# Weights by column blocks, token ids by one small matmul, and a setup order rewritten

## The chip, the cores and the metric

The kernel runs on one core of a Trainium2 chip, in float32. The metric is the device time of one launch in microseconds (us), as the median of several runs. TensorE (PE) multiplies, VectorE (DVE) and ScalarE (ACT) move and convert, GpSimd (POOL) selects small tables and issues gathers, SyncE (SP) issues the plain transfers.

## What is computed

`x` is [64, 64, 512]: 64 tokens of 64 rows. Four stages follow each other, each added to its input. Token b picks its adapter in each stage by an id of its own.

```python
x = x + x @ W_base.T + scaling[e0] * (((x @ Wt.T) @ A0[e0].T) @ B0[e0].T) @ Wp.T    # e0: 4 adapters of rank 16
x = x + x @ W1.T     + scalings[e1] * ((x @ A1[e1].T) @ B1[e1].T)                   # e1: 8 adapters of rank 16
x = x + einsum('bct,bcd->bdt', x, w2[e2])                                            # e2: 8 matrices 64x64
x = x + einsum('bct,bcd->bdt', x, w3[e3])                                            # e3: 200 matrices 64x64
```

## The kernel before

**Two phases.** The setup (about the first 38 us) folds the weights of the first two stages into one 512x512 matrix `g01` and small tables. Then eight turns of four token pairs follow (`PAIRS` = 32, `QUAD` = 4, `QUADS` = 8). A turn multiplies w2 and w3 of its tokens (`token_mix`), applies the product to x (`mix`, result `y_ps`), reads it to `y_all` and splits it into a rounded float32r half and a remainder (`yy`), multiplies both with `g01` (`apply`, 12 matmuls for a pair), reduces to rank rows (`reduce`) and adds the adapters' part (`close`), which reads rows `v_sel` gathered from the HBM table `v_table`.

**The folding.** `g1` is (W1 + 1) transposed on PE: 16 transposes of 128x128 blocks of `w1_sb`, into four banks `g1_0` to `g1_3`. POOL first adds the unit matrix to each diagonal block (L353, and L348 for `wb_sb`, which is W_base). ACT reads each bank as a rounded high half, DVE subtracts it to get the low half (`low_g1`). W_base is split in the same way (`wb_high_k`, `wb_low_k`). `g01` sums over four k: step k needs `g1_k` and `wb_k`, high and low, and is 12 matmuls of 512 columns (4 high x high, 8 mixed); step 0 begins with its four high x high.

Between the steps stand the transposes of Wp (`wpT`), of A1, A0 and w2, the products `vu` (which need the 1 MB transfer of Wt), `gu1T`, `cross`, `v0g1` and four matmuls `v_0` to `v_3`, whose results DVE sums into `v_tab`. One SP transfer writes `v_tab` to `v_table`.

**Order.** Nothing is scheduled by a tool. Each engine has its list, written by hand, and waits on semaphores. `setup_ps`, `setup_act` and `setup_dve` count the finished setup steps of PE, ACT and DVE; `ORDER` names the PSUM bank of each PE result, `ACT_STEPS` and `DVE_STEPS` the order of the readers. An engine stands still behind a wait, with everything that its list has behind it. SP's list is one queue of transfers. `keep_warm(16)` is 16 transposes of the unit matrix into a bank that is not read.

**Token ids.** Ids e3, e0 and e1 are copied to all 128 partitions by transfers that repeat the row 128 times (`ids`), and e0, e1, e2 once more to one partition (`code_ids`). DVE makes gather rows for w3 (`find_w3_rows`), table rows (`find_v_rows`) and packed codes, six linked small operations.

Of the kernel before, what the change touches and what calls it, by code (L numbers as in the profile page):

```python
# [40 lines left out]
def build(nc, x, e0_ids, e1_ids, e2_ids, e3_ids, w_base, w_t, a0, b0, w_p, s0, w1, a1, b1, s1, w2, w3, out):  # L41
# [995 lines left out]
```

## Time and profile before

| | us |
|---|---|
| median of 3 runs | 172.2 (171.82 to 172.25) |
| the profiled execution | 172.37 |
| its span in the trace | 170.2 |
| PE busy | 163.6 (96% of the span) |
| DVE / POOL / ACT busy | 91.1 / 86.7 / 48.5 |
| TensorE clock granted, mean | 0.997 |

The span runs from the first to the last recorded event; 2.2 us of the execution lie outside it. A busy PE is not PE at its peak, since ends of matmuls are modelled: PE times below are differences of starts.

### The profile page before, as it was taken

What the parts mean: (1) busy time and instruction counts of PE and PEld (TensorE: products, weight loads), DVE (VectorE), ACT (ScalarE), POOL (GpSimd) and SP (SyncE); (2) the same over time, 40 slices, a digit from 0 to 9 for tenths busy, and PEclk for the clock granted to TensorE, in tenths of its full rate; (3) what the DMA queues carried; (4) which work ended last, traced back from release to release, by engine and by line L of the source; (5) the groups of instructions that cost most, each with busy time, mean ns of one, the idle gap of its engine ahead of it and who ended that gap; (6) DMA issues with size and microseconds to landing.
All of it is one profiled execution on the core that took longest, in us unless ns stands there. A gap on an engine that the chain in (4) does not pass through costs nothing.

```text
span 170.2 us, 6468 instructions
## 1 busy us (share of the span) xinstructions
PE 163.6 (96%) x2348; PEld 125.0 (73%) x2348; DVE 91.1 (54%) x212; ACT 48.5 (28%) x96; POOL 86.7 (51%) x194
## 2 busy tenths in 40 slices
PE   5889999999999999999999999999999999999992
PEld 5669467678786878687868886877778687868761
DVE  4195975899770846263636645563666180617010
ACT  3142426244230602240223024220503060214021
POOL 4410477764675648475737674756454053608200
PEclk9999999999999999999999999999999999999998
DMA  4799942119550594077309531953394059006406
GB/s 141 252 329 321 282 177 85 33 60 331 190 192 27 168 322 145 23 208 293 131 15 294 209 137 70 285 178 116 123 311 161 31 155 337 2 0 250 123 9 242
DMA packets 16614, 28.75 MB, mean 169 GB/s; under 512 B 3862, under 2 KB 3990, under 8 KB 16598
## 3 DMA queue, kind: packets, MB, share of 16 engines
q1 hardware_dynamic: 14294, 23.31, 41.8%
q0 software_dynamic: 2304, 5.25, 9.1%
q8 instruction: 8, 0.13, 0.3%
q14 instruction: 8, 0.07, 0.1%
HBM read 18.85 MB, written 9.70 MB: 168 GB/s over the span
## 4 chain that ended last, share of the span: by engine, by line
PE 91%; DMA 3%; DVE 1%; SPq 1%; issue 1%; ACT 1%; POOL 0%; DVEq 0%
PE o_ps L751 65%; PE y_ps L751 12%; PE z_ps L751 8%; DMA wb_sb<-in_L_cond_W_base_dram 3%; PE p_ps L751 3%; PE y_ps L764 1%; SPq L231 1%; PE y_ps L811 1%; DVE g L552 0%; PE p_ps L853 0%; DVE b_by L546 0%; ACT o_sb L486 0%; PE p_ps L824 0%; PE z_ps L811 0%; PE p_ps L811 0%
## 5 line engine op out<-in xcount | busy, mean ns | idle before, releaser
L751 PE MATMUL o_ps<-g,yy 128*128 128x512 f32 x384 | 92.1, 395 | 0.0
L751 PEld LDWEIGHTS o_ps<-g,yy 128*128 128x128 f32 x384 | 70.8, 188 | 16.1 <-issue 0.8
L339 POOL COPY u_sel<-u_tab 128x64 f32 x128 | 32.3, 258 | 41.3 <-PE z_ps L751 31.5
L318 POOL DMA_INDIRECT w_all<-in_L_cond_weights_dram,w_rows x32 | 31.8, 994 | 9.6 <-issue 9.6
L631 DVE COPY y_all<-y_ps 128x512 f32<-128x512 f32 x32 | 20.6, 686 | 15.0 <-PE y_ps L751 14.9
L673 DVE COPY o_sb<-o_ps 128x512 f32<-128x512 f32 x15 | 9.7, 687 | 34.5 <-PE o_ps L751 34.5
L426 ACT ACTIVATE yy<-y_all 128x512 fp32r<-128x512 f32 x32 | 19.7, 632 | 16.5 <-DVE y_all L631 16.1
L638 DVE TENSOR_TENSOR yy<-y_all,yy 128x512 fp32r<-128x512 f32 x32 | 21.2, 701 | 3.0 <-ACT yy L426 2.7
L327 POOL DMA_INDIRECT v_sel<-v_table,v_rows x16 | 17.5, 1094 | 6.2 <-issue 6.2
L445 ACT ACTIVATE o_sb<-o_ps 128x512 f32<-128x512 f32 x16 | 8.7, 595 | 37.9 <-PE o_ps L751 37.9
L751 PE MATMUL y_ps<-p_now,x_raw 64*64 64x64 f32 x1024 | 18.6, 221 | 0.0
L665 DVE COPY w_sel<-w2T 64x64 f32 x56 | 12.5, 222 | 10.6 <-issue 7.2
L751 PEld LDWEIGHTS y_ps<-p_now,x_raw 64*64 64x64 f32 x1024 | 16.4, 134 | 1.7 <-DVE v_tab L552 0.4
L751 PEld LDWEIGHTS z_ps<-y_all,u_sel 128*32 128x32 f32 x512 | 8.0, 109 | 9.0 <-issue 9.0
L439 ACT ACTIVATE z<-z_ps 128x64 f32<-128x64 f32 x16 | 3.6, 227 | 34.8 <-PE z_ps L751 34.8
L751 PE MATMUL o_ps<-g,wb 128*128 128x512 f32 x48 | 12.2, 400 | 1.0 <-ACT g L389 0.8
L751 PEld LDWEIGHTS o_ps<-g,wb 128*128 128x128 f32 x48 | 8.7, 188 | 4.1 <-ACT g L389 1.0
L751 PE MATMUL z_ps<-y_all,u_sel 128*32 128x64 f32 x512 | 10.5, 222 | 0.0
L751 PE MATMUL o_ps<-v_sel,z 32*64 32x512 f32 x128 | 8.9, 613 | 0.0
L348 POOL TENSOR_TENSOR wb_sb<-wb_sb,ident 128x128 f32<-128x128 f32 x4 | 2.1, 514 | 10.6 <-DMA wb_sb<-in_L_cond_W_base_dram 10.6
L792 PE MATMUL o_ps<-ident 128*128 128x128 f32 x16 | 3.7, 421 | 1.8 <-POOL ident L306 1.8
L432 ACT ACTIVATE p_now<-p_ps 128x256 f32<-128x256 f32 x8 | 3.1, 385 | 5.4 <-PE p_ps L751 5.3
(115 smaller groups left out, 104.5 us busy)
## 6 DMA issues: line engine op xcount, KB each, us to landing
x_raw<-in_x_dram SPq DMA_DIRECT2D x16, 512.0 KB, 4.7
out_dram<-o_sb SPq DMA_DIRECT2D x14, 512.0 KB, 5.4
w_sb<-in_L_cond_W_dram SPq DMA_DIRECT2D x4, 256.0 KB, 3.6
wb_sb<-in_L_cond_W_base_dram SPq DMA_DIRECT2D x4, 256.0 KB, 7.1
wp_sb<-in_L_cond_Wp_dram SPq DMA_DIRECT2D x2, 512.0 KB, 6.3
wt_sb<-in_L_cond_Wt_dram SPq DMA_DIRECT2D x1, 1024.0 KB, 8.9
v_table<-v_tab SPq DMA_DIRECT2D x1, 1024.0 KB, 5.7
out_dram<-o_sb SPq DMA_DIRECT2D x4, 256.0 KB, 2.3
```

The lines of the kernel that those rows point to most:

```text
L318: pool.indirect_dma_start(out=w3_all[:, j, :], out_offset=None, in_=w3_flat, in_offset=bass.IndirectOffsetOnAxis(ap=w3_rows[:, j:j + 1], a ...
L327: pool.indirect_dma_start(out=v_sel[:, h, :], out_offset=None, in_=v_table, in_offset=bass.IndirectOffsetOnAxis(ap=v_rows[:, h, i:i + 1], ...
L339: nc.gpsimd.tensor_copy(u_sel[u][:, :, b, RANK * part:RANK * part + RANK], u_tab[:, :, bass.ds(e, 1), :].rearrange("p k a r -> p k (a r)") ...
L426: nc.scalar.activation(yy[u][:, :, 0, :], y_all[u % 2][:, :, :], ACT.Copy).then_inc(yh_set, 1)
L439: nc.scalar.activation(z[:, h, :], z_ps[:, 0:SEQ], ACT.Copy).then_inc(z_set, 1)
L445: nc.scalar.activation(o_sb[:, u, :], o_ps[u][:, :], ACT.Copy).then_inc(o_set, 1)
L631: nc.vector.tensor_copy(y_all[u % 2][:, :, :].rearrange("p k (b t) -> p b k t", b=2), y_of(u)).then_inc(yf_set, 1)
L638: nc.vector.tensor_tensor(yy[u][:, :, 1, :], y_all[u % 2][:, :, :], yy[u][:, :, 0, :].bitcast(F32), ALU.subtract).then_inc(yl_set, 1)
L665: nc.vector.tensor_copy(to[rows, u, :], w2T[rows, bass.ds(g, 1), :].rearrange("p a c -> p (a c)")).then_inc(w2_placed, 1)
L673: nc.vector.tensor_copy(o_sb[:, u, :], o_ps[u][:, :]).then_inc(o_set_dve, 1)
L751: return nc.tensor.matmul(dst, lhsT, rhs, start=start, stop=stop)
L792: nc.tensor.transpose(o_ps[3][:, 0:PART], ident[:, :], ident[:, :])
```

## The change

W1 is loaded by blocks of 128 columns (four blocks, each in all four row groups) in place of blocks of 128 rows. So the four transposes that make `g1_0` need one transfer, not four. PE's list then alternates: transposes of block k, and the g01 step that they allow. `keep_warm` has 11 transposes, not 16.

The four id rows come by four transfers of 256 bytes each, issued from ACT's queue. DVE turns them to float32r, PE multiplies a column of ones with them (one matmul with one contraction row and 256 columns, into `z_ps`), and DVE copies the result to `ids` on all partitions. The repeated transfers are gone.

`g01_step(2)` stands ahead of `vu`. For it the third block of W_base is loaded behind Wp, POOL's `plus_wb(2)` and `plus_wb(3)` stand between the gathers, and ACT's and DVE's work on `wb` 2 comes earlier. `mix(0)` of the first turn and half of step 3 stand ahead of the `v` matmuls, whose DVE sums now run 3, 2, 1, 0 and behind the first reads of `y_ps`. The core of the diff:

```diff
-        ACT_STEPS = ["g1_0", "g1_1", "wb_high_1", "g1_2", "g1_3", "wpT_0", "wpT_2", "a1T", "wb_high_2", "wb_high_3",
...
+        ACT_STEPS = ["g1_0", "g1_1", "wb_high_1", "g1_2", "g1_3", "wpT_0", "wpT_2", "wb_high_2", "a1T", "wb_high_3",
...
-                     "v_2", "v_1", "v_0", "v_3",
+                     "v_3", "v_2", "v_1", "v_0",
...
-            w1_rows = w1.rearrange("(c p) d -> p c d", p=PART)
+            w1_rows = w1.rearrange("(c p) (k d) -> p k c d", p=PART, d=PART)
...
-            for c in range(KC):
-                sp.dma_start(w1_sb[:, c, :], w1_rows[:, c, :]).then_inc(w1_in[c], 16)
-            for k in range(2):
-                load_wb(k)
-            sp.dma_start(ids[:, 2, :], e3_ids.partition_broadcast(PART)).then_inc(e3_in, 16)
-            for n, t in enumerate((e0_ids, e1_ids, e2_ids)):
-                sp.dma_start(code_ids[:, n, :], t.partition_broadcast(1)).then_inc(code_in, 16)
+            for k in range(KC):
+                sp.dma_start(w1_sb[:, k, :, :], w1_rows[:, k, :, :]).then_inc(w1_in[k], 16)
+                if k < 2:
+                    load_wb(k)
...
-            sp.dma_start(s0_sb[:, :], s0.partition_broadcast(PART)).then_inc(b0_in, 16)
-            sp.dma_start(b0_sb[:, :, :, :], b0.rearrange("e (p s) r -> p e s r", s=KC)).then_inc(b0_in, 16)
+            load_wb(2)
...
+            sp.dma_start(s0_sb[:, :], s0.partition_broadcast(PART)).then_inc(b0_in, 16)
+            sp.dma_start(b0_sb[:, :, :, :], b0.rearrange("e (p s) r -> p e s r", s=KC)).then_inc(b0_in, 16)
...
-            for k in range(2, KC):
-                load_wb(k)
...
             sp.dma_start(b1_sb[:, :, :, :], b1.rearrange("e (p s) r -> p e s r", s=KC)).then_inc(b1_in, 16)
-            for n, t in enumerate((e0_ids, e1_ids)):
...
+            sp.wait_ge(setup_dve, DVE_DONE["v_0"])
             sp.dma_start(v_table[0:EF * RANK, :].rearrange("(g p) d -> p g d", p=PART), v_tab[:, :, :]).then_inc(table_out, 16)
...
-            for c in range(KC):
-                pool.wait_ge(w1_in[c], 16)
-                blk = w1_sb[:, c, PART * c:PART * c + PART]
...
+                pool.wait_ge(w1_in[k], 16)
+                blk = w1_sb[:, k, k, :]
                 nc.gpsimd.tensor_tensor(blk, blk, ident[:, :], ALU.add).then_inc(w1_plus, 1)
...
-                plus_wb(k)
-            for k in range(2, KC):
-                plus_wb(k)
+                if k < 2:
+                    plus_wb(k)
             pool.wait_ge(rows_set, 1)
-            gather_w3(range(0, W3_FIRST - 1))
+            gather_w3(range(0, 3))
+            plus_wb(2)
+            gather_w3(range(3, 5))
+            plus_wb(3)
+            gather_w3(range(5, W3_FIRST - 1))
 
             pool.wait_ge(code_set, 1)
...
+            for n, t in enumerate((e0_ids, e1_ids, e2_ids, e3_ids)):
+                act.dma_start(ids_row[:, n, :], t.partition_broadcast(1)).then_inc(ids_in, 16)
...
                 read_g1(k)
-            for s in range(0, KC, 2):
-                read(f"wpT_{s}", wpT[:, s, :], bank_of(f"wpT_{s}"))
+            read("wpT_0", wpT[:, 0, :], bank_of("wpT_0"))
+            read("wpT_2", wpT[:, 2, :], bank_of("wpT_2"))
+            high_wb(2)
             read("a1T", a1T[:, 0, :, :].rearrange("p k r -> p (k r)"), bank_of("a1T"))
-            for k in range(2, KC):
-                high_wb(k)
+            high_wb(3)
...
             for k in range(2):
                 read_g01(k)
-            high_y(0, 0)
-            read_g01(2)
             high_y(0, 1)
-            read_g01(3)
+            for k in range(2, KC):
+                read_g01(k)
             turn(0, first=True)
             with act.Fori(1, QUADS - 1) as i:
...
             nc.vector.tensor_copy(wb[:, 0, 0, :], wb_sb[:, 0, :]).then_inc(setup_dve, 1)
             low_wb(0)
-            for k in range(2):
-                low_g1(k)
+            low_g1(0)
+            dve.wait_ge(ids_spread, 1)
+            nc.vector.tensor_copy(ids[:, :, :].rearrange("p n b -> p (n b)"), z_ps[:, 0:4 * BATCH]).then_inc(ids_set, 1)
+            dve.wait_ge(ids_set, 1)
+            find_w3_rows()
+            low_g1(1)
             low_wb(1)
-            for k in range(2, KC):
-                low_g1(k)
-            find_w3_rows()
-            scale(E0, b0_in, b0_sb, b0_now, s0_sb)
-            dve.wait_ge(code_in, 48)
-            link(nc.vector.scalar_tensor_tensor(out=code_part[:, 0, :], in0=code_ids[:, 1, :], scalar=float(E0),
-                                                in1=code_ids[:, 0, :], op0=ALU.mult, op1=ALU.add))
+            low_g1(2)
...
+            low_g1(3)
...
             for s in range(1, KC, 2):
                 copy(f"wpT_{s}", wpT[:, s, :], bank_of(f"wpT_{s}"))
...
             copy("a0T", a0T[:, :, :].rearrange("p k r -> p (k r)"), bank_of("a0T")[:, 0:KC * R0])
             read_low("a1T", a1T[:, 1, :, :].rearrange("p k r -> p (k r)"), bank_of("a1T"),
...
             def copy_y(i, u):
...
+            place_w2(1, w2_next)
...
+            add_w3(1, w3_next)
+            find_v_rows()
             dve.wait_ge(setup_act, ACT_DONE["v0g1"])
             read("v0g1", v0g1[0:R0, :], bank_of("v0g1")[0:R0, :], v0g1_low[:, :], ALU.add)
-            add_w3(1, w3_next)
-            find_v_rows()
+            for u in range(2):
+                copy_y(0, u)
+            low_y(0, 0)
             dve.wait_ge(setup_act, ACT_DONE["v0g1_both"])
-            for g in (2, 1, 0, 3):
+            for g in (3, 2, 1, 0):
...
 
-            for u in range(2):
-                copy_y(0, u)
-            low_g01(0)
...
-                if k == 0:
-                    pe.wait_ge(setup_act, ACT_DONE["g1_0"])
-                    pe.wait_ge(setup_dve, DVE_DONE["wb_high_0"])
-                    for t in range(KC):
-                        g01_part(0, t, ((0, 0),))
...
-            keep_warm(16)
-            for c in range(KC):
-                pe.wait_ge(w1_plus, c + 1)
-                for k in range(KC):
+            keep_warm(11)
+            def flip_w1(k):
+
+                pe.wait_ge(w1_plus, k + 1)
+                for c in range(KC):
                     last = nc.tensor.transpose(bank_of(f"g1_{k}")[:, PART * c:PART * c + PART],
-                                               w1_sb[:, c, PART * k:PART * k + PART], ident[:, :])
-                    if c == KC - 1:
-                        last.then_inc(setup_ps, 1)
+                                               w1_sb[:, k, c, :], ident[:, :])
+                last.then_inc(setup_ps, 1)
+
+            flip_w1(0)
+            pe.wait_ge(ids_f_set, 2)
+            mm(z_ps[:, 0:4 * BATCH], ones_row[:, :], ids_f[:, :, :].rearrange("p n b -> p (n b)"),
+               True, True).then_inc(ids_spread, 1)
+            g01_high()
+            flip_w1(1)
             g01_step(0)
+            flip_w1(2)
             g01_step(1)
+            pe.wait_ge(ids_set, 1)
+            flip_w1(3)
...
+            g01_step(2)
...
+                if first:
+                    pe.wait_ge(setup_dve, DVE_DONE["v_1"])
                 mix(1)
+                if first:
+                    pe.wait_ge(setup_dve, DVE_DONE["v_0"])
...
-            g01_step(2)
-
-            pe.wait_ge(p_set, 1)
+            pe.wait_ge(setup_act, ACT_DONE["gu1"])
+            mix_ready(0, 0)
+            mix(0)
+            g01_step(3, range(0, 2))
+
+            pe.wait_ge(yf_set, 2)
...
-            g01_step(3, range(0, 2))
-            pe.wait_ge(setup_dve, DVE_DONE["v_1"])
-            mix_ready(0, 0)
-            mix(0)
             g01_step(3, range(2, KC))
...
```

PE's rows at the start of the program, of before. `g` is g1, `w_sb` is w1_sb, `o_ps` are the banks of g01:

```order
L792 MATMUL o_ps<-ident 128x128 x16
L799 MATMUL y_ps<-ident,w_sb 128x128
L799 MATMUL p_ps<-ident,w_sb 128x128
...
L799 MATMUL y_ps<-ident,w_sb 128x128
L799 MATMUL z_ps<-ident,w_sb 128x128
L751 MATMUL o_ps<-g,wb 128x512 x24
L811 MATMUL y_ps<-ident,wp_sb 128x128 x4
```

The same place of the change:

```order
L803 MATMUL o_ps<-ident 128x128 x11
L811 MATMUL y_ps<-ident,w_sb 128x128 x4
L760 MATMUL z_ps<-ids_f,ones_row 128x256
L760 MATMUL o_ps<-g,wb 128x512 x4
L811 MATMUL p_ps<-ident,w_sb 128x128 x4
L760 MATMUL o_ps<-g,wb 128x512 x8
L811 MATMUL y_ps<-ident,w_sb 128x128 x4
L760 MATMUL o_ps<-g,wb 128x512 x12
L811 MATMUL z_ps<-ident,w_sb 128x128 x4
L832 MATMUL y_ps<-ident,wp_sb 128x128 x4
```

The 16 transposes no longer stand in one piece ahead of the 24 matmuls, and the small ids matmul stands behind the first four.

DVE's rows from the end of `find_row_shift` on, of before:

```order
L523 TENSOR_SCALAR row_shift<-row_shift 32x1
L580 CAST wb<-wb_sb 128x512
L566 TENSOR_TENSOR wb<-wb_sb,wb 128x512
L552 TENSOR_TENSOR g<-y_ps,g 128x512
L552 TENSOR_TENSOR g<-p_ps,g 128x512
L557 TENSOR_TENSOR wb<-wb_sb,wb 128x512
L552 TENSOR_TENSOR g<-y_ps,g 128x512
L552 TENSOR_TENSOR g<-z_ps,g 128x512
L504 TENSOR_SCALAR lane<-lane 64x32
L505 SCALAR_TENSOR_TENSOR w_rows<-ids,lane 64x32
```

And of the change:

```order
L525 TENSOR_SCALAR row_shift<-row_shift 32x1
L586 CAST ids_f<-ids_row 1x256
L588 CAST wb<-wb_sb 128x512
L568 TENSOR_TENSOR wb<-wb_sb,wb 128x512
L554 TENSOR_TENSOR g<-y_ps,g 128x512
L592 CAST ids<-z_ps 128x256
L506 TENSOR_SCALAR lane<-lane 64x32
L507 SCALAR_TENSOR_TENSOR w_rows<-ids,lane 64x32
L506 TENSOR_SCALAR lane<-lane 64x32
L507 SCALAR_TENSOR_TENSOR w_rows<-ids,lane 64x32
L554 TENSOR_TENSOR g<-p_ps,g 128x512
L559 TENSOR_TENSOR wb<-wb_sb,wb 128x512
```

Two casts are new, one of them ahead of the first work on `wb`, and the four operations for the w3 rows moved ahead of the low halves that step 1 needs.

PE's rows between `v0g1` (its last row first) and the first turn, of before and with the change:

```order
L751 MATMUL o_ps<-g,wb 128x512 x12
L751 MATMUL p_ps<-v,cross 128x512
L751 MATMUL y_ps<-v,cross 128x512 x2
L751 MATMUL z_ps<-v,cross 128x512
L751 MATMUL o_ps<-g,wb 128x512 x6
L751 MATMUL y_ps<-p_now,x_raw 64x64 x32
L751 MATMUL o_ps<-g,wb 128x512 x6
L751 MATMUL z_ps<-y_all,u_sel 32x64 x16
```

```order
L760 MATMUL y_ps<-p_now,x_raw 64x64 x32
L760 MATMUL o_ps<-g,wb 128x512 x6
L760 MATMUL p_ps<-v,cross 128x512
L760 MATMUL y_ps<-v,cross 128x512 x2
L760 MATMUL z_ps<-v,cross 128x512
L760 MATMUL o_ps<-g,wb 128x512 x6
L760 MATMUL z_ps<-y_all,u_sel 32x64 x16
```

Step 2 (x12) is gone from here, and `mix(0)` (x32) stands ahead of the `v` matmuls.

## Rows read from the trace of the kernel before

**Rows 1.** The page: the chain that ended last, by engine, in shares of the span.

```profile
PE 91%; DMA 3%; DVE 1%; SPq 1%; issue 1%; ACT 1%; POOL 0%; DVEq 0%
```

**Rows 2.** PE's timeline: start, us, engine, line, operation, [idle before].

```profile
1.77 3.67 PE L792 MATMUL o_ps<-ident 128*128 128x128 f32 x16 [1.77 <-POOL ident L306]
5.24 0.36 PE L799 MATMUL y_ps<-ident,w_sb 128*128 128x128 f32 x1
...
8.84 1.17 PE L751 MATMUL o_ps<-g,wb 128*128 128x512 f32 x4 [0.80 <-ACT g L389]
10.21 4.84 PE L751 MATMUL o_ps<-g,wb 128*128 128x512 f32 x20 [0.20 <-DVE g L552]
14.88 0.64 PE L811 MATMUL y_ps<-ident,wp_sb 128*128 128x128 f32 x4
...
16.82 0.99 PE L764 MATMUL y_ps<-ident,a_sb 128*128 128x128 f32 x8
...
30.24 2.89 PE L751 MATMUL o_ps<-g,wb 128*128 128x512 f32 x12
...
35.71 1.19 PE L751 MATMUL y_ps<-p_now,x_raw 64*64 64x64 f32 x64
```

**Rows 3.** DVE's timeline, same columns.

```profile
4.70 0.15 DVE L523 TENSOR_SCALAR row_shift<-row_shift 32x1 f32<-32x1 f32 x1
8.27 0.43 DVE L580 CAST wb<-wb_sb 128x512 fp32r<-128x512 f32 x1 [3.42 <-POOL wb_sb L348]
8.73 0.83 DVE L566 TENSOR_TENSOR wb<-wb_sb,wb 128x512 fp32r<-128x512 f32 x1
9.48 0.68 DVE L552 TENSOR_TENSOR g<-y_ps,g 128x512 fp32r<-128x512 f32 x1
10.08 0.68 DVE L552 TENSOR_TENSOR g<-p_ps,g 128x512 fp32r<-128x512 f32 x1
...
12.47 0.16 DVE L504 TENSOR_SCALAR lane<-lane 64x32 int32<-64x32 int32 x1
13.09 0.19 DVE L505 SCALAR_TENSOR_TENSOR w_rows<-ids,lane 64x32 int32<-64x32 int32 x1
...
17.85 0.42 DVE L611 COPY a0T<-y_ps 128x256 f32<-128x256 f32 x1
```

**Rows 4.** POOL's and ACT's timeline, same columns.

```profile
3.60 1.06 POOL L353 TENSOR_TENSOR w_sb<-w_sb,ident 128x128 f32<-128x128 f32 x2 [1.48 <-DMA w_sb<-in_L_cond_W_dram]
6.20 0.45 POOL L353 TENSOR_TENSOR w_sb<-w_sb,ident 128x128 f32<-128x128 f32 x1 [1.55 <-DMA w_sb<-in_L_cond_W_dram]
20.13 1.10 POOL L318 DMA_INDIRECT w_all<-in_L_cond_weights_dram,w_rows  x1 [0.17 <-issue]
...
7.75 0.60 ACT L389 ACTIVATE g<-y_ps 128x512 fp32r<-128x512 f32 x1 [5.65 <-PE y_ps L799]
```

**Rows 5.** SP's timeline (issues), and time to landing of W1 and of `ids`.

```profile
0.82 1.82 SPq L231 DMA_DIRECT2D w_sb<-in_L_cond_W_dram  x4
...
DMA to landing us min/median/max: 2.7/3.6/4.6
...
DMA to landing us min/median/max: 5.7/5.9/8.2
```

**Rows 6.** Stretches of 0.5 us: busy of PE, PEld, DVE, ACT, POOL; clock; DMA share; GB/s.

```profile
14.00:14.50 0.50, 0.50 (x4) 0.42 (x3) 0.43 (x3) 0.00 (x0) 0.00 (x0) 1.00 1.05 182
15.50:16.00 0.50, 0.50 (x7) 0.50 (x6) 0.00 (x0) 0.44 (x1) 0.00 (x0) 1.00 1.05 389
```

**Rows 7.** The table `v_table`: SP's write, POOL's second gather, its reader, landings.

```profile
36.88 0.36 SPq L278 DMA_DIRECT2D v_table<-v_tab  x1
44.99 0.95 POOL L327 DMA_INDIRECT v_sel<-v_table,v_rows  x1 [0.31 <-issue]
53.60 1.11 PE L751 MATMUL o_ps<-v_sel,z 32*64 32x512 f32 x16
...
DMA to landing us min/median/max: 3.4/3.8/5.1
```

More of the change, by code:

```diff
@@ L64, in build @@
         owner = sb("owner", [PART, E1])
-        ids = sb("ids", [PART, 3, BATCH], I32)
-        code_ids = sb("code_ids", [1, 3, BATCH], I32)
+        ids = sb("ids", [PART, 4, BATCH], I32)
+        ids_row = sb("ids_row", [1, 4, BATCH], I32)
+        ids_f = sb("ids_f", [1, 4, BATCH], F32R)
+        ones_row = sb("ones_row", [1, PART], F32R)
+        one = sb("one", [1, PART])
         code_part = sb("code_part", [1, 3, BATCH], I32)
@@ L84, in build @@
         first = ExitStack()
-        w1_sb = sb("w1_sb", [PART, KC, D], of=first)
+        w1_sb = sb("w1_sb", [PART, KC, KC, PART], of=first)
         wp_sb = sb("wp_sb", [PART, KC, D], of=first)
@@ L505, in find_w3_rows @@
                     last = nc.vector.scalar_tensor_tensor(
-                        out=w3_rows[half, :], in0=ids[half, 2, :].rearrange("p (j b) -> p b j", b=2)[:, b],
+                        out=w3_rows[half, :], in0=ids[half, 3, :].rearrange("p (j b) -> p b j", b=2)[:, b],
                         scalar=float(SEQ), in1=lane64[half, :], op0=ALU.mult, op1=ALU.add)
@@ L577, in _ @@
                 nc.vector.tensor_copy(ident2[half, :], ident[half, half]).then_inc(ident2_set, 1)
+            nc.vector.memset(one[:, :], 1.0).then_inc(code_step, 1)
+            steps[0] += 1
+            dve.wait_ge(code_step, steps[0])
+            nc.vector.tensor_copy(ones_row[:, :], one[:, :]).then_inc(ids_f_set, 1)
             find_row_shift()
+            dve.wait_ge(ids_in, 64)
+            nc.vector.tensor_copy(ids_f[:, :, :], ids_row[:, :, :]).then_inc(ids_f_set, 1)
             dve.wait_ge(wb_plus, 1)
@@ L581, in _ @@
             low_wb(0)
-            for k in range(2):
-                low_g1(k)
-            low_wb(1)
-            for k in range(2, KC):
-                low_g1(k)
-            find_w3_rows()
-            scale(E0, b0_in, b0_sb, b0_now, s0_sb)
-            dve.wait_ge(code_in, 48)
-            link(nc.vector.scalar_tensor_tensor(out=code_part[:, 0, :], in0=code_ids[:, 1, :], scalar=float(E0),
-                                                in1=code_ids[:, 0, :], op0=ALU.mult, op1=ALU.add))
+            low_g1(0)
+            dve.wait_ge(ids_spread, 1)
+            nc.vector.tensor_copy(ids[:, :, :].rearrange("p n b -> p (n b)"), z_ps[:, 0:4 * BATCH]).then_inc(ids_set, 1)
+            dve.wait_ge(ids_set, 1)
+            find_w3_rows()
+            low_g1(1)
+            low_wb(1)
+            low_g1(2)
+            link(nc.vector.scalar_tensor_tensor(out=code_part[:, 0, :], in0=ids_row[:, 1, :], scalar=float(E0),
+                                                in1=ids_row[:, 0, :], op0=ALU.mult, op1=ALU.add))
             ef = code_part[:, 0, :].rearrange("p (j b) -> p b j", b=2)
@@ L622, in _ @@
                 read("w2T", w2T[SEQ * b:SEQ * b + SEQ, :, :].rearrange("p g (a j) -> p g a j", j=W2J), w2_bank, eye, ALU.add)
-            for k in range(2, KC):
-                low_wb(k)
+            low_wb(3)
             def copy_y(i, u):
@@ L721, in low_g01 @@
                 read_low(f"g01_{t}", g01[:, 1, t, :], bank_of(f"g01_{t}"), g01[:, 0, t, :])
-            for u in range(2):
-                copy_y(0, u)
-            low_g01(0)
-            low_y(0, 0)
-            for k in range(1, KC):
+            for k in range(KC):
                 low_g01(k)
@@ L773, in g01_part, with g01_high @@
                 return last
-            def g01_step(k, blocks=range(KC)):
-                if k == 0:
-                    pe.wait_ge(setup_act, ACT_DONE["g1_0"])
-                    pe.wait_ge(setup_dve, DVE_DONE["wb_high_0"])
-                    for t in range(KC):
-                        g01_part(0, t, ((0, 0),))
+            def g01_high():
+                pe.wait_ge(setup_act, ACT_DONE["g1_0"])
+                pe.wait_ge(setup_dve, DVE_DONE["wb_high_0"])
+                for t in range(KC):
+                    g01_part(0, t, ((0, 0),))
+            def g01_step(k, blocks=range(KC)):
                 pe.wait_ge(setup_dve, max(DVE_DONE[f"g1_{k}"], DVE_DONE[f"wb_low_{k}"]))
```

20 lines of the change are left out of this document (11 added, 9 removed), and 2 rows, old and new, of the table ORDER.

## The prediction

> **What bounds the kernel now.** I read the page first. It has PE busy for 163.6 of 170.2 us, 96%, and the chain that ended last is 91% PE [rows 1]. So whatever moves PE's first unbroken stretch moves the end, one for one, as long as no new hole opens behind it; work saved on other engines is worth nothing by itself.
>
> The second view is PE's timeline, to find where that stretch begins. PE works on `keep_warm` from 1.77 and on the first W1 transpose from 5.24; after the transposes it stands 0.80 us for ACT, then again for DVE, and from 10.21 it runs on without a hole that matters [rows 2]. The 20 matmuls from 10.21 end steps 0 and 1 at 10.21 + 4.84 = 15.05: 0.242 us each. Between 5.24 and 10.21 PE had to do only 16 transposes and 4 matmuls. A transpose costs 0.121 us once PE is fast ((16.82 - 14.88)/16 [rows 2]), so that is 1.94 + 0.97 = 2.9 us of work in 4.97 us. About 2 us are open there. The cause stands in POOL's rows: the third W1 block is ready for its unit matrix only at 6.20 [rows 4], each bank of g1 needs all four, then ACT takes 0.60 for the first bank (7.75 [rows 4]), and DVE, which waited until 8.27 for W_base, delivers the low half of `g1_0` at 10.16 (9.48 + 0.68 [rows 3]).
>
> **The change at the start.** I follow PE and DVE through the new lists with the old durations.
>
> PE: `keep_warm` took (5.24 - 1.77)/16 = 0.217 us each [rows 2]; 11 of them end at 1.77 + 2.39 = 4.16. The first W1 block gets its unit matrix from 3.60 on, in 0.45 us [rows 4], so it is there. Four transposes at the slow spacing end at 5.03.
>
> DVE: the row_shift chain ended at 4.85 (4.70 + 0.15 [rows 3]). A memset and a small cast ahead of it cost some 0.2 each, like the small rows there: 5.25. The cast of 256 ids on one partition I put at 0.35, between 0.16 for 32 columns and 0.42 for 256 on all partitions [rows 3]: 5.60. `wb_high_0` takes 0.46 to the next start (8.27 to 8.73), `wb_low_0` 0.75 (8.73 to 9.48), `g1_0` 0.68: 6.06, 6.81, 7.49 [rows 3]. Its bank is read by ACT from about 5.2 to 5.8, so DVE does not wait. The copy of the ids to `ids` is a copy of 256 columns, 0.42; the four w3 row operations take 13.28 - 12.47 = 0.81; the low halves of `g1_1` and `wb` 1 take 0.60 and 0.68 [rows 3]. With the overlap of 0.08 after `g1_0` and 0.05 for the semaphore: 7.83, 8.70, 9.30, 9.98.
>
> PE again: after 5.03 it waits for the ids cast until 5.6, multiplies (256 columns and one contraction row: between nothing and one 512-column matmul, 0.24; I take 0.15) and waits for `wb_high_0` until 6.1. Four matmuls end at 7.07, four transposes at 7.55 (second W1 block third in the queue, the place that landed just ahead of 6.20 [rows 4]). Step 0 may start at 7.5: its eight end at 9.49, transposes at 9.97. Step 1 waits for DVE's 9.98: 12 matmuls end at 12.9, the last transposes at 13.4. Before, the same work ended at 15.05. **Gain: 15.05 - 13.4 = 1.65 us.** The three holes that are left (5.03 to 6.1, and slivers) are DVE's: what binds is DVE's list of small work, not W1.
>
> **The change further on.** (a) `g01_step(2)`, 12 matmuls, moves from 30.24 [rows 2] to ahead of `vu`. It adds and removes 2.9 us, so it costs nothing if `wb_low_2` is ready. PE comes there at 13.4 + 1.94 for Wp + 12 x 0.121 = 16.8. ACT reads `g1_3` until 14.1, `wpT_0` until 14.7, `wpT_2` (whose transposes end at 14.95) until 15.55, then `wb_high_2` until 16.15, at 0.60 each [rows 4]; DVE follows with 0.68: 16.9. A wait of 0.1 to 0.2. On POOL `plus_wb(2)` stands behind three gathers. They used to start at 20.13 [rows 4]; with rows ready at 8.7 and about 1.25 each (1.10 and the pause to the next) it ends near 13. Without that cover every microsecond would fall on step 2. The move also gives Wt, 1 MB behind Wp in SP's queue, 2.9 us more before `vu` needs it.
>
> (b) `mix(0)` ahead of the `v` matmuls: they now wait for DVE's two reads of `y_ps` (`yf_set` 2). After `v0g1` PE has 1.1 for the mix (35.71, 1.19 [rows 2]) and 6 x 0.242 for half of step 3, 2.6 in all; DVE needs 1.2 until the mix is done and two reads at 0.6 to 0.68, 2.6 to 2.7. A wait of 0.1. Queued behind it are the `v` sums, the low halves of g01 and so the first `apply`; they have over 0.6 us in hand each, since `apply` begins only after reduce, mix and token matmuls.
>
> (c) The table: from v0g1's end (30.24) to SP's write of `v_tab` (36.88 [rows 7]) were 6.6 us with step 2's 2.9 in them; now 3.7 + 1.1 + 1.45 = 6.3, from an end that lies at 30.24 + 2.9 - 1.4 = 31.7. So the write goes out at 38.0, 1.1 later. The second gather shifts from 44.99 to 46.1 and lands 3.8 to 5.1 us later [rows 7], at 51.2 at the latest; `close` reads it at 53.60 - 1.4 = 52.2. It costs nothing, with 1 us left.
>
> Fewer repeated transfers, other positions of small loads, the reversed `v` sums: they lie beside PE. The turns from 45 us on are untouched.
>
> **Sum:** 1.65 - 0.15 - 0.1 = 1.4 us. The profiled execution took 172.37 with a span of 170.2; I expect a span of 168.8, and against the median of 172.2, which is 0.17 below that execution, 170.8.
>
> **W1 in pieces of 512 bytes** has no row here. Below: no cost, the forecast. Above: in a stretch where 256-byte pieces were moved the rate was 182 GB/s, in one of 2 KB pieces 389 [rows 6]; a block of 262 KB then takes 1.44 in place of 0.67. The second W1 block has itself and one W1 block in that state: it lands 1.5 later, its transposes start at 8.2 and not at 7.07, and 1.1 us of the gain goes: 171.9. I take no cost, since up to 0.45 us of lateness of that block is free (6.2 + 0.45 against 7.07), and pieces of 512 bytes are nearer to 2 KB in what they carry per piece than those 256-byte ones.
>
> The Trainium skill, "DMA: Bandwidth & Descriptors", Why small descriptors are slow, gives a fixed overhead of about 3 cycles per packet beside one for each 32 bytes. An estimate from that page: 4 x 19 cycles against 67, 13% more, under 0.1 us for a block. By it the sum stays 1.4; by the stretch at 182 GB/s it would be 0.3.
>
> **The rivals.**
>
> *Ids arrive late (slower).* DVE now waits for four id rows before its first work on W_base, and everything above hangs on DVE's list. They are issued on ACT's queue, about 0.82 + 3 x 0.46 = 2.2 for the last, by SP's issue times [rows 5]. With the quickest landing, 2.7 [rows 5], they are there at 4.9, ahead of 5.25. With the 5.7 that the repeated `ids` took at the least [rows 5] they come at 7.9: 2.65 late, 173.4. It decides from a landing at 6.65 on (gain gone), 4.4 us after issue. For it: the DMA engines are nearly full then. Against: `ids` stood behind 1.5 MB in its own queue, these stand behind nothing.
>
> The Trainium skill, same page, Issuing engines are not separate DMA queues, speaks against the change here: transfers of all engines share 16 DMA engines and interleave, and a second issuer saves only issue time.
>
> *PE stays slow.* Equal transposes were 0.217 apart before 5.24 and 0.121 later [rows 2], the spacing of the 1.2 and the 2.4 GHz level. The new list has a hole of about 1 us just where PE became fast. If the first four matmuls and the second transposes also run slow: 0.97 + 0.48 more, less the little that DVE's waits absorb, 1.1: 171.9; with step 0 slow too, over 173. Against it: the holes of 0.80 and 0.20 us up to 10.21 [rows 2] did not slow PE down.
>
> The Trainium skill, "TensorE: Matmul & The Clock Gate", What's actually happening, says that the clock is halved by default and that activity releases it; the two spacings agree.
>
> *The wait only moves.* If step 2 or the table comes over 1 us late, the start's gain is given back there: 171.8 to 172.2.
>
> *Holes close.* With no DVE wait PE would be through at 5.03 + 7.4 = 12.4: a gain of 2.6. Half of that more than forecast gives 170.2.
>
> **Chances.** Forecast 62%. Holes smaller 5%. W1 slow by pieces 12%, in two thirds of it still faster. PE slow 10%, the wait moves 3%, ids late 8%. A measurement here tells about 0.3%, 0.5 us, from no change. Faster 0.62 + 0.05 + 0.08 = 0.75; same 0.04 + 0.08 + 0.03 = 0.15; slower 0.08 + 0.02 = 0.10. The range goes from 169.9 (holes closed in good part) to 172.1 (both prices that end at 171.9), and leaves out late ids.
>
> **What would show it.** Right: first g01 matmul near 6.1, step 1 near 10.0, Wp's transposes from 13.4, `vu` near 19.8, first `reduce` 1.4 us earlier than before, and PE full from 10 on. Wrong: DVE's ids cast later than 6 (ids late); the transposes of W1's second block at 0.2 us spacing (slow); a POOL wait for W1's second block beyond 7 (pieces); PE waits ahead of step 2, the `v` matmuls or the first `close`.

## The result and the profile after

Slower, by 1.0%. The changed kernel took 173.87 us (median of 6 runs, 173.25 to 174.46) against 172.22 (171.67 to 172.69), ratio 1.0096 with a 95% interval of 1.0066 to 1.0126. Timed once more (`again`) it was 173.19 in 9 runs, ratio 1.0060 (1.0031 to 1.0088). 170.8 was forecast. The profiled execution took 173.25 with a span of 171.3, where a span of 168.8 was forecast.

The page first: the chain that ended last, which was 91% PE before [rows 1].

```profile
PE 84%; DVE 5%; DMA 4%; issue 3%; DVEq 1%; POOL 1%; ACT 0%; POOLq 0%
```

PE still carries it, but DVE has 4 points more, issue 2 and DMA 1: there are new waits on the path. PE's timeline shows where (the rows that answer to [rows 2], and the two first `reduce`):

```profile
1.77 2.61 PE L803 MATMUL o_ps<-ident 128*128 128x128 f32 x11 [1.77 <-POOL ident L304]
4.17 1.11 PE L811 MATMUL y_ps<-ident,w_sb 128*128 128x128 f32 x4
5.42 0.58 PE L760 MATMUL z_ps<-ids_f,ones_row 1*128 1x256 f32 x1
5.98 2.07 PE L760 MATMUL o_ps<-g,wb 128*128 128x512 f32 x4
7.85 1.05 PE L811 MATMUL p_ps<-ident,w_sb 128*128 128x128 f32 x4
8.55 2.59 PE L760 MATMUL o_ps<-g,wb 128*128 128x512 f32 x8
10.98 0.60 PE L811 MATMUL y_ps<-ident,w_sb 128*128 128x128 f32 x4
11.34 3.00 PE L760 MATMUL o_ps<-g,wb 128*128 128x512 f32 x12
...
14.61 0.65 PE L832 MATMUL y_ps<-ident,wp_sb 128*128 128x128 f32 x4
...
18.33 3.04 PE L760 MATMUL o_ps<-g,wb 128*128 128x512 f32 x12
...
28.67 0.63 PE L876 MATMUL p_ps<-ident,b_by 128*128 128x128 f32 x4 [0.28 <-DVE b_by L548]
...
38.53 0.65 PE L760 MATMUL z_ps<-y_all,u_sel 128*32 128x64 f32 x32
...
47.13 0.65 PE L760 MATMUL z_ps<-y_all,u_sel 128*32 128x64 f32 x32 [0.63 <-DMA x_raw<-in_x_dram]
```

Rows of the kernel before for the same places:

```profile
25.80 0.63 PE L853 MATMUL p_ps<-ident,b_by 128*128 128x128 f32 x4 [0.22 <-DVE b_by L546]
...
38.44 0.65 PE L751 MATMUL z_ps<-y_all,u_sel 128*32 128x64 f32 x32
...
46.25 0.65 PE L751 MATMUL z_ps<-y_all,u_sel 128*32 128x64 f32 x32
```

The ids matmul and the first g01 matmul come about when forecast (5.6 and 6.1). But four g01 matmuls go from 5.98 to 7.85, 0.47 each, where they took 0.242 before: the spacing of the 1.2 GHz level. "Slow level" and "fast level" below mean these two spacings. Step 0 has two matmuls more at that spacing ((10.98 - 8.55) - 8 x 0.242 = 0.5). Step 1 begins at 11.34, not at 10.0, and Wp's transposes at 14.61, not at 13.4. The first `reduce` starts at 38.53; before it was 38.44.

The same list at the fast level stands in the profile of `again` (172.48 us, span 170.5):

```profile
6.13 1.19 PE L760 MATMUL o_ps<-g,wb 128*128 128x512 f32 x4 [0.38 <-ACT g L392]
9.80 3.01 PE L760 MATMUL o_ps<-g,wb 128*128 128x512 f32 x12
13.09 0.64 PE L832 MATMUL y_ps<-ident,wp_sb 128*128 128x128 f32 x4
...
27.69 0.63 PE L876 MATMUL p_ps<-ident,b_by 128*128 128x128 f32 x4 [0.82 <-DVE b_by L548]
37.55 0.65 PE L760 MATMUL z_ps<-y_all,u_sel 128*32 128x64 f32 x32
...
46.37 0.65 PE L760 MATMUL z_ps<-y_all,u_sel 128*32 128x64 f32 x32 [0.85 <-DMA x_raw<-in_x_dram]
```

Here the start is as forecast, Wp at 13.09, 1.8 us ahead of before, and yet the time is 172.5 and the first `reduce` only 0.9 ahead. Two waits take most of it back: 0.82 us for `b_by` and 0.85 for x ahead of the second `reduce`.

**The wait for `b_by`** is explained by DVE's timeline of the changed kernel:

```profile
23.00 1.63 DVE L675 COPY w_sel<-w2T 64x64 f32 x6 [0.44 <-issue]
25.27 2.20 DVE L675 COPY w_next<-w2T 64x64 f32 x8 [0.64 <-issue]
27.50 0.42 DVE L554 TENSOR_TENSOR v0T<-y_ps,v0T 128x256 fp32r<-128x256 f32 x1
27.84 0.68 DVE L548 TENSOR_TENSOR b_by<-b_sb,s_sb 128x512 f32<-128x512 f32 x1
```

`place_w2(1, w2_next)`, eight copies in 2.2 us and 0.6 of issue ahead of them, stood behind `cross` before (from 28.91) and stands ahead of `vuT` (`v0T` in the row) and `b_by` now. PE's four transposes of `b_by` wait behind it.

**The wait for x** is explained by SP's timeline:

```profile
39.75 0.36 SPq L276 DMA_DIRECT2D v_table<-v_tab  x1
40.15 9.28 SPq L253 DMA_DIRECT2D x_raw<-in_x_dram  x3
```

Before, the load went out at 37.29:

```profile
37.29 3.33 SPq L255 DMA_DIRECT2D x_raw<-in_x_dram  x2
```

The write of `v_tab` waits for `v_0` and goes out 2.9 us later than before [rows 7]. The load of the second turn's x stands behind it in SP's list, and behind its 1 MB in the queue: it went out at 40.15 and PE could use it at 47.13, 7.0 us later. The median x load of this run took 4.7 to land; that the 1 MB ahead makes the difference is argued from this and not tested by itself.

The difference of the two spans from 168.8, by stretches of PE's path: the start of Wp, from there to the first `reduce`, to the second, to the end. The forecast for them is 13.4, 23.8 (23.56 before, and the two waits of 0.15 and 0.1 that it allowed), 7.8 and 124.0 (both as before). The forecast took 1.65 from 15.05, the end of the matmuls ahead, where Wp's row starts at 14.88; so its span of 168.8 is 0.17 shorter than these four add up to.

| | start of Wp | to `reduce` 1 | to `reduce` 2 | to the end | span over 168.8 |
|---|---|---|---|---|---|
| changed kernel | 14.61 | 23.92 | 8.60 | 124.2 | 2.5 |
| `again` | 13.09 | 24.46 | 8.82 | 124.1 | 1.7 |

### The profile page after: what moved, and what is told of

Read it like the earlier page. It is cut to its first block, busy times and chain, and to the rows that moved or that the text cites. A ratio compares the mean times of both kernels' runs of the same rounds, so it can differ in the third digit from the quotient of the medians.

```text
span 171.3 us, 6464 instructions
## 1 busy us (share of the span) xinstructions
PE 165.3 (96%) x2344; PEld 125.4 (73%) x2344; DVE 90.7 (53%) x216; ACT 48.7 (28%) x96; POOL 86.4 (50%) x194
## 4 chain that ended last, share of the span: by engine, by line
PE 84%; DVE 5%; DMA 4%; issue 3%; DVEq 1%; POOL 1%; ACT 0%; POOLq 0%
PE o_ps L760 61%; PE y_ps L760 10%; PE z_ps L760 8%; DMA x_raw<-in_x_dram 4%; PE p_ps L760 3%; DVEq L675 1%; PE y_ps L832 1%; DVE row_shift L522 1%; DVE w_sel L675 1%; PE p_ps L811 0%; DVE w2T L554 0%; DVE wb L559 0%; PE z_ps L832 0%; DVE wpT L620 0%; PE p_ps L876 0%
## 5 line engine op out<-in xcount | busy, mean ns | idle before, releaser
L337 POOL COPY u_sel<-u_tab 128x64 f32 x128 | 32.9, 260 | 47.1 <-PE z_ps L760 34.9
L325 POOL DMA_INDIRECT v_sel<-v_table,v_rows x16 | 16.6, 1036 | 9.8 <-issue 5.6
L675 DVE COPY w_sel<-w2T 64x64 f32 x56 | 11.5, 204 | 11.4 <-issue 6.5
L760 PE MATMUL o_ps<-g,wb 128*128 128x512 f32 x48 | 14.0, 438 | 0.0
L760 PEld LDWEIGHTS o_ps<-g,wb 128*128 128x128 f32 x48 | 9.5, 209 | 3.1 <-issue 0.8
L760 PE MATMUL p_ps<-w_now,w_sel 64*64 64x64 f32 x112 | 4.6, 219 | 0.0
L803 PE MATMUL o_ps<-ident 128*128 128x128 f32 x11 | 2.6, 426 | 1.8 <-POOL ident L304 1.8
```

Source lines behind the costliest of these rows:

```text
L325: pool.indirect_dma_start(out=v_sel[:, h, :], out_offset=None, in_=v_table, in_offset=bass.IndirectOffsetOnAxis(ap=v_rows[:, h, i:i + 1], ...
L337: nc.gpsimd.tensor_copy(u_sel[u][:, :, b, RANK * part:RANK * part + RANK], u_tab[:, :, bass.ds(e, 1), :].rearrange("p k a r -> p k (a r)") ...
L675: nc.vector.tensor_copy(to[rows, u, :], w2T[rows, bass.ds(g, 1), :].rearrange("p a c -> p (a c)")).then_inc(w2_placed, 1)
L760: return nc.tensor.matmul(dst, lhsT, rhs, start=start, stop=stop)
```

## The experiments

Theory after the result: three causes, (L) PE's level in the first 9 us differs from launch to launch and the new list has no slack there, (B) the `w2_next` copies ahead of `b_by`, (X) the x load behind the table's write. Rivals: the level comes from the shorter `keep_warm`; the waits are harmless.

**`again`, `e1_keep16`, `e2_x_first`, `e3_filled`**, on one chip, with the kernel before at 172.45. The edits:

```diff
-            keep_warm(11)                       # e1
+            keep_warm(16)
...
+            load(1, 0)                          # e2: ahead of the write of v_tab
             sp.wait_ge(setup_dve, DVE_DONE["v_0"])
             sp.dma_start(v_table[0:EF * RANK, :]...
-            load(1, 0)
...
+            keep_warm(3)                        # e3: around the ids matmul
             pe.wait_ge(ids_f_set, 2)
...
+            keep_warm(3)
             g01_high()
```

> The changed kernel once more, for a second profile. Its first profiled execution took 173.25 us, the fastest of its six, while their median is 173.87. Theory A (PE at half speed until about 8.9 us, by when the level happens to rise, plus a wait of 0.63 us for x in turn 0): the first four g01 matmuls again near 0.47 us apart, the first reduce near 38.5, and again a wait for x of 0.6 us or more ahead of the second reduce; the time 173.3 to 174.5. Rival B (the slow stretch was an accident of that one execution): the four matmuls near 0.24 us apart and the first reduce near 37.2, and then the 0.6 us between profile and median would be something else still.

> The changed kernel with 16 warming transposes as before, not 11. Theory A1 (PE is slow because it paused at 5 us, after 3.3 us of work; with 16 it works without a pause until 5.7 like the kernel before, and is fast from 5.3 on): the g01 high matmuls 0.24 apart, steps 0 and 1 done near 13.4 to 13.8, first reduce 0.7 to 0.9 earlier than in the changed kernel although W1's transposes start 1.1 later; time 0.7 to 0.9 below the changed kernel's. Rival A2 (what slows PE is the small ids matmul or the many short waits, not the number of warming transposes): the high matmuls still 0.47 apart, time 0.3 to 1.1 above the changed kernel's.

> The changed kernel with one line moved in SP's list: the load of x for turn 1, first half, stands ahead of the write of v_tab and not behind it. Theory C (the second reduce waits for this load, which now queues behind a write of 1 MB that goes out 2.9 us later than before): that wait of 0.63 us is gone, the time is 0.6 to 1.2 below the changed kernel's, about 172.9. Rival D (the wait only moves: the table comes later and the first close waits for the gathered rows): the wait reappears at the first close and the time is the same within 0.3.

> The changed kernel with 11 warming transposes, and three more behind the first four W1 transposes and three behind the ids matmul, so that PE has no pause until the g01 high matmuls. Theory A1 (the pause at 5 us is what keeps PE slow): the high matmuls 0.24 apart, steps 0 and 1 done near 13.2, time 1.0 to 1.3 below the changed kernel's. Rival A2 (the pause plays no part): the high matmuls stay 0.47 apart, time the same or up to 0.3 above.

Measured: again 1.0060 (1.0031 to 1.0088); e1 173.22 us, 1.0048 (1.0024 to 1.0072); e2 172.95, 1.0018 (0.9992 to 1.0043); e3 173.01, 1.0031 (1.0001 to 1.0062). With 16 warming transposes the profile still shows 0.47 us spacing, and g01 1.0 us later than in the changed kernel (from 6.98): 16 transposes don't ensure the fast level. Whether they make it likelier one profile can't say. e3's profile was at the fast level and cost its six transposes 0.5 (g01 from 6.62); a single profile doesn't say whether the filling helped. e2's profile has no wait for x:

```profile
35.14 0.37 SPq L253 DMA_DIRECT2D x_raw<-in_x_dram  x1
40.46 0.37 SPq L277 DMA_DIRECT2D v_table<-v_tab  x1
```

```profile
29.38 0.63 PE L876 MATMUL p_ps<-ident,b_by 128*128 128x128 f32 x4 [0.77 <-DVE b_by L548]
39.24 0.65 PE L760 MATMUL z_ps<-y_all,u_sel 128*32 128x64 f32 x32
...
47.12 0.65 PE L760 MATMUL z_ps<-y_all,u_sel 128*32 128x64 f32 x32
```

From reduce to reduce it needs 7.88 where the changed kernel needed 8.60. X is right by the row; in time the interval of e2 still overlaps that of `again`.

**`e5_before_keep11`, `e6_place_late`, `e7_place_x`, `e8_step2_back`.** e5 is the kernel before with `keep_warm(11)`. e6 undoes B, e7 is e6 with e2's edit, e8 puts `g01_step(2)` back behind `v0g1`:

```diff
             place_w2(0)                         # e6, e7
-            place_w2(1, w2_next)
...
             add_w3(0)
+            find_v_rows()
...
                                     ALU.subtract).then_inc(setup_dve, 1)
-            add_w3(1, w3_next)
-            find_v_rows()
+            place_w2(1, w2_next)
             dve.wait_ge(setup_act, ACT_DONE["v0g1"])
...
             low_y(0, 0)
+            add_w3(1, w3_next)
```

> The kernel before with 11 warming transposes, not 16. Three profiles of changed kernels showed PE at half speed until about 9 us (11 or 16 warming transposes alike) and two showed it fast from 5.3 us on. Theory A (when PE becomes fast differs from execution to execution, and the old list has 2 us of slack ahead of 10.2 that covers most of it): time within 0.3 us of the kernel before, whichever the profile shows. Rival A3 (the five transposes fewer are what delays the faster level): the profile shows PE slow until 9, and the time is 0.5 us or more above before.

> The changed kernel with DVE's selection of w2 for turn 1 back behind the cross products, as before, and the table rows computed ahead of them, where DVE stood idle for 1.3 us. Theory E (the eight copies of 2.2 us ahead of the low half of vuT delay b1's scaling, and PE waits 0.3 to 0.8 for it): that wait falls to under 0.1, no new one above 0.2 appears, time 0.3 to 0.8 below the changed kernel's 173.4. Rival F (PE's gain only runs into the x load, which lands at a time of its own): the wait for x ahead of the second reduce grows by what is saved, time the same within 0.3.

> Both: w2's selection back behind the cross products and x's load ahead of v_tab's write. If both waits are real and nothing else is behind them, 1.1 to 1.6 below the changed kernel, 171.8 to 172.3, that is 0.1 to 0.4% below the kernel before; where the profile falls on an execution with PE fast from 5.3 us, its span is near 168.9 (170.5 of the fast profile less 0.8 and 0.85). If the first close then waits for the gathered rows, 172.5 or more.

> The changed kernel with the third step of g01 back behind v0g1. Theory G (the third step ahead of vu is needed to cover the transfer of Wt, which lands near 18, and DVE's low half of W_base): PE waits 1 to 2.5 us ahead of vu, and more for b1's scaling since DVE's list is then 2.9 us nearer: time 1 us or more above the changed kernel. Rival H (the early third step gives nothing): time the same or lower, with PE's waits ahead of vu under 0.5.

Measured: e5 172.53, 1.0014 (0.9988 to 1.0039); e6 174.15, 1.0091 (1.0055 to 1.0127); e7 172.03, 0.9985 (0.9961 to 1.0008); e8 177.98, 1.0315 (1.0282 to 1.0349). e5's profile is at the slow level until past 8.4 us, and its g01 matmuls begin at 8.83 all the same; it has Wp at 15.15, 0.3 later than before, and took 172.59. That shows the old list's slack. It is also what the rival of a shorter `keep_warm` expects of the profile, though not of the time. e6 alone gains nothing:

```profile
27.35 0.63 PE L876 MATMUL p_ps<-ident,b_by 128*128 128x128 f32 x4 [0.22 <-DVE b_by L548]
35.05 0.69 PE L760 MATMUL p_ps<-v,cross 32*128 32x512 f32 x1 [0.42 <-DVE y_all L641]
...
37.72 0.65 PE L760 MATMUL z_ps<-y_all,u_sel 128*32 128x64 f32 x32
...
46.68 0.65 PE L760 MATMUL z_ps<-y_all,u_sel 128*32 128x64 f32 x32 [1.04 <-DMA x_raw<-in_x_dram]
```

Its copies now stand ahead of `y_all`, which costs the `v` matmuls 0.42. That is where B's 0.6 went: from Wp to `b_by` e6 is 0.6 shorter than `again` (13.98 against 14.60), from the mix to the `v` matmuls 0.5 longer (3.17 against 2.68), and from Wp to the first `reduce` only 0.1 shorter (24.35 against 24.46). So the wait for `b_by` has gone and its price stays on the path in another place. With x loaded first as well (e7) the 1.04 are gone too: from `reduce` to `reduce` e7 takes 7.88 and e6 8.96. e6 and e7 are one list but for that load, and their intervals don't touch. The medians are 2.1 apart and overstate it, since five of e6's eight times are above 174, where L puts its slow launches. By their profiles at the fast level (172.58 and, run again, 172.35 against 171.75 and 171.19) x is worth 1.0: the x wait is shown. e8 shows what the early step 2 is worth in this list: without it PE waits 0.82 for `a0T` ahead of `vu`, 2.43 for `b_by` and 1.40 for x.

```profile
19.20 0.61 PE L760 MATMUL z_ps<-wpT,b_now 128*64 128x512 f32 x1 [0.82 <-DVE a0T L620]
28.72 0.63 PE L874 MATMUL p_ps<-ident,b_by 128*128 128x128 f32 x4 [2.43 <-DVE b_by L548]
```

**`e9_rows_late`** is e7 with `find_w3_rows` behind `low_wb(1)`:

```diff
-            dve.wait_ge(ids_set, 1)
-            find_w3_rows()
             low_g1(1)
             low_wb(1)
+            dve.wait_ge(ids_set, 1)
+            find_w3_rows()
```

> The kernel with both repairs (w2's selection late, x's load ahead of the table's write), and DVE's four operations for the w3 rows behind the low halves of g1_1 and wb 1. In its fast profile PE stood 0.5 us ahead of step 1 for these halves (transposes of block 2 at 9.29, step 1 at 10.03 and not at 9.65). Theory I (that wait is DVE's list): step 1 starts within 0.1 us of the transposes' end, the median 0.2 to 0.4 below 172.0. Rival (the halves wait for ACT, or the gathers, now 1.3 us later, hold up w_now): step 1 no earlier, time the same or a new wait ahead of the first token matmul.

Measured: 173.11, 1.0035 (1.0011 to 1.0059). Its 12 times form two groups: 171.56 to 171.73, and 172.32 to 173.64. The profile (171.61, fast level, Wp at 13.20) is of the first group and no better than e7's two at this level (13.34 and 13.07): there is no gain from the DVE order that I had taken for the bound of the start. DVE's low half of `g1_1` now waits 1.29 for ACT, as that run's rival had it.

On the same chip both kernels were profiled once more, the kernel before twice: `before_a` and `before_b` (173.16, 172.78; W1's transposes at the fast spacing from 6.1 and from 4.95, Wp at 14.40 and 14.71) and `again_b` (173.77; g01 0.47 apart, Wp at 14.80). The two of before say one thing more. Wp starts up to 0.5 earlier than in the first profile, yet the first `reduce` stands at 39.21 and 38.74, not at 38.44: PE waits 0.90 and 0.24 for Wt and 0.64 and 0.62 for `b_by`. So an earlier start of Wp is no gain by itself in the old list, and the 0.22 for `b_by` of the first profile is not fixed.

What made the two groups was open. Four more runs asked whether it is L; the rival (R) is that the times don't go with the spacing.

> Edit: e7_place_x with keep_warm of 1 transpose in place of 11, so PE is idle from about 2 us until the first W1 block. Theory L (each launch finds PE either at the 0.121 us spacing from about 5 us on, or at 0.21 us until about 9 us; the new list has no slack there): now every launch is of the slow kind, the first eight W1 transposes and the first four g01 matmuls are 0.21 and 0.47 apart, Wp's transposes start at 14.6 to 15.3 in place of 13.4, and the times form ONE group near 173.2 to 173.8, with few or none near 171.7. Rival R (the spread of e7_place_x and e9_rows_late has another cause, DMA or POOL): the times keep both groups or stay at a median of 172.0, whatever the spacing in the profile.

> e7_place_x once more. Theory L: times in two groups, near 171.6 and near 173.1, or between as the shares fall; if the profile has g01's first four matmuls 0.47 apart, its time is 172.8 or more, if 0.24 apart 172.2 or less. Rival R: one group near 172.0, and the profile's time doesn't go with its spacing.

> e7_place_x, one look. Theory L: profile with first g01 matmuls 0.24 apart at 172.2 or less, with 0.47 apart at 172.8 or more. Rival R: no such link.

> e6_place_late once more, one look. Theory L: 0.24 apart gives 172.4 to 172.9 as in its first profile, 0.47 apart gives 173.9 to 174.5, the group in which most of its launches fell; b_by wait 0.2 and x wait near 1.0 in either case. Rival R: a time near 174.2 with 0.24 spacing, or near 172.6 with 0.47.

The profiles of e7_b (171.19 us) and of e7_c (173.60), the same kernel on the same chip:

```profile
4.33 1.11 PE L811 MATMUL y_ps<-ident,w_sb 128*128 128x128 f32 x4
...
6.13 1.19 PE L760 MATMUL o_ps<-g,wb 128*128 128x512 f32 x4 [0.35 <-ACT g L392]
...
9.80 3.00 PE L760 MATMUL o_ps<-g,wb 128*128 128x512 f32 x12
...
13.07 0.65 PE L832 MATMUL y_ps<-ident,wp_sb 128*128 128x128 f32 x4
...
37.45 0.65 PE L760 MATMUL z_ps<-y_all,u_sel 128*32 128x64 f32 x32
```

```profile
4.27 1.12 PE L811 MATMUL y_ps<-ident,w_sb 128*128 128x128 f32 x4
...
6.07 2.07 PE L760 MATMUL o_ps<-g,wb 128*128 128x512 f32 x4
...
11.71 3.00 PE L760 MATMUL o_ps<-g,wb 128*128 128x512 f32 x12
...
14.99 0.65 PE L832 MATMUL y_ps<-ident,wp_sb 128*128 128x128 f32 x4
...
39.36 0.65 PE L760 MATMUL z_ps<-y_all,u_sel 128*32 128x64 f32 x32
```

Both begin alike at 4.3. From there one is 1.92 us ahead at Wp and 1.91 at the first `reduce`; the times are 2.4 apart, and the last 0.4 to 0.5, behind the second `reduce`, is not explained. e6_b had 0.24 spacing and took 172.35, as L has it. e10_cold, which is e7 with `keep_warm(1)`, had 0.47 spacing in its profile (g01 from 6.04, Wp from 15.03) and has one group of times, 172.86 to 174.34 with a median of 173.24 (1.0051, 1.0032 to 1.0070), where e7 beside it went from 171.19 to 174.58 (median 172.80, 1.0008, 0.9981 to 1.0036). In all six profiles of e6, e7 and e9 and in e10 the time goes with the spacing as L has it, so R is out. The groups are not sharp, though: e7 and its repeat have times from 172.04 to 172.82 too, which no profile covers.

**`e11_before_cold`, `e12_before_cold`**: the kernel before with `keep_warm(1)`, to see whether the old list can afford the slow level.

> Edit: the kernel before with keep_warm of 1 transpose in place of 16. Theory L: the old list can afford the slow level, since its first g01 matmuls wait for the transfers and ACT anyway. So it is slow in every launch (W1 transposes 0.21 apart until past 8 us) and still 172.4 to 172.9, at most 0.5 us over before, in one group; the same edit's slow level costs the new list 1.5 to 1.9 at Wp's transposes, here at most 0.5 (Wp at 15.0 to 15.4 against 14.88). Rival R (the slow level costs every list the same): 173.7 or more, and Wp's transposes at 16.3 or later.

> e11_before_cold once more (the old list with keep_warm of 1), since its first timing fell on a chip on which the kernel before itself took 179.75 us with a spread of 3. Theory L: at most 0.5 us over before, Wp's transposes at 15.4 at the latest. Rival R: 1.3 us or more over before, Wp's transposes at 16.3 or later.

e11 came to a chip on which the kernel before took 179.75 us, so only its start is read: transposes 0.21 apart until past 8 us, and still Wp at 14.48. e12: 173.06 against 172.58, 1.0018 (0.9992 to 1.0045), times from 171.48 to 174.03.

```profile
8.41 7.71 PE L751 MATMUL o_ps<-g,wb 128*128 128x512 f32 x24
15.96 0.64 PE L811 MATMUL y_ps<-ident,wp_sb 128*128 128x128 f32 x4
```

That is neither what L expected (15.4 at most) nor R's 16.3: the 24 matmuls took 7.55 where 5.81 would be full speed, so some seven of them ran at 0.47, up to about 11.8 us, and the old list lost 1.1 at Wp. The old list has slack against slow transposes, since its g01 matmuls begin at 8.4 to 8.8 anyway; it has none against slow g01 matmuls. Nor does `keep_warm(1)` put all launches at one place: e11's level rose at about 9 us and e12's at 11.8, and e12's times are 2.5 apart, which L as two fixed moments doesn't explain.

## Why the prediction was wrong, by its steps

**"PE again ... Four matmuls end at 7.07, ... transposes at 13.4"**: this step assumed the fast level from 5.03 on. It failed in 6 of the 13 profiles of the new list and its variants (e10_cold, where it was forced, not counted), the changed kernel's own among them, and what came instead was the rival *PE stays slow*, put at 10%. In the seven with 0.24 us spacing Wp starts at 13.07 to 13.85, so the size of the start's gain was right for them. The wait was not: the first g01 matmul stood 0.38 for ACT's read of `g1_0` (`again`, `g L392`), not for DVE's work on W_base, and step 1 followed its transposes without a hole. That the two came out equally long is luck. In the others it is 14.6 to 15.8. The argument against the rival, that holes of 0.80 and 0.20 us had not slowed PE down, was of no use: nothing fell here, the level rose later. The price was put at 1.1 with step 0 at full speed. With two to four of step 0's matmuls slow as well, it is 1.5 (changed kernel) to 1.9 (e7). I had one profile of before and read its level as a property of the list.

**"(c) The table ... costs nothing with 1 us left"**: the span from `v0g1`'s end to the write was forecast at 6.3 and is 6.55 (33.20 to 39.75), and no `close` waited for the table. What failed is that I followed the moved write and not what stands behind it in SP's list. By my own 38.0 the load would have gone at 38.4, and with 7.0 it comes at 45.4, 0.5 after the second `reduce` of the forecast (46.25 - 1.4 = 44.9). Measured: 0.6 to 1.0 in the changed list.

**"Fewer repeated transfers ... they lie beside PE"** counted edits as covered and never named the move of `place_w2(1)`. It costs 0.6 where PE is on time (0.82 in `again` against the 0.22 of e6), and little where PE is late (0.28 in the changed kernel). No run gave it back in time: e6, which undoes it, pays 0.5 elsewhere.

**Right:** ids in time (cast at 5.08), W1 in pieces of 512 bytes at no cost that shows (POOL had the second block at 5.39), so neither of those rivals; step 2 early without a wait of its own; the `v` matmuls not late by more than 0.1 in the changed kernel. The Trainium skill, "DMA: Bandwidth & Descriptors", Why small descriptors are slow, gives about 3 cycles of overhead per packet, from which the prediction estimated under 0.1 us for a block. The rows don't isolate it: a W1 block took 3.8 us to land at the median, 4.4 in `again` and 3.6 before, and PE stood for none of them there.

One slip of the sums that changed nothing: with all holes closed the forecast's own numbers give 169.9, and half of that extra gain 170.3, not 170.2.

**The sum in place of mine**, an estimate from these rows: on the forecast's 170.8 come X 0.6 to 1.0, B 0.6, and L 1.5 in about half of the launches (6 of 13 profiles), which with B and X behind it is partly absorbed (the profiles of the changed kernel at either level are 1.5 apart at Wp and 0.8 at the end, since a PE that is late waits less for `b_by`). That is 172.0 to 172.4 at the fast level and 172.8 to 173.9 at the other; profiles of the changed kernel gave 172.48, and 173.25 and 173.77. e7, without X and with B's wait only moved, gives 171.2 to 171.8 at the fast level: the forecast plus the 0.4 that its `v` matmuls wait, and up to 0.6 more. In the median e7 isn't told from before (0.9985 and 1.0008). No version here beats the kernel before.

**Open:** why the level rises before 6.1 us in one launch and past 9 in another of the same kernel, and whether 16 warming transposes make the early rise likelier. The one profile of e1 says only that they don't ensure it. The old list was fast by 6.1 in all three profiles with 16 and slow past 8 in the one with 11, which speaks for it; the median of e1, 173.22 against 173.19, speaks against it. B alone was not told from noise in time, only in rows, and a place for the copies that delays neither `b_by` nor `y_all` was not tried.

## What to carry to other kernels

When a wait moves on a queue engine, follow every instruction behind it, with the bytes ahead of it in the queue: the load behind a late write was the loss here, not the write. Undoing a wait by moving work back can only move the wait: e6 freed `b_by` of 0.6 us and put 0.5 in front of the `v` matmuls. So compare the stretches between fixed points, not the one wait. A schedule that takes the slack out of the first microseconds wins only in launches where PE is already fast; look at more than one profile before you take an early spacing as given.

## What the hardware showed beside this

The granted clock in the profile's windows does not show the level of the start. Busy time, counts and clock (1.00 in both, the third value from the end) in 6 to 9 us, the changed kernel and then `again`:

```profile
6.00:9.00 3.00, 3.00 (x9) 2.51 (x10) 2.41 (x7) 0.06 (x1) 1.86 (x5) 1.00 1.09 348
```

```profile
6.00:9.00 3.00, 2.87 (x15) 2.39 (x16) 2.81 (x8) 1.19 (x3) 1.74 (x4) 1.00 1.09 357
```

9 matmuls (transposes included) against 15, with PE busy 3.00 and 2.87 us: only the spacing of equal matmuls (0.47 or 0.24) tells it. The Trainium skill, "TensorE: Matmul & The Clock Gate", What's actually happening, has the clock halved until activity releases it, and says that the moment varies from run to run of one kernel. The spacings agree: e7's list was fast by 6.13 us in one launch and slow past 8.65 in another.

A load of 0.5 MB issued 0.4 us behind a write of 1 MB on one queue was usable 6.9 to 7.7 us after its issue (e3 and e8 the ends, eight profiles); the median x load of the changed kernel landed after 4.7.
